# Half-swapped q and k by a partition shuffle out of PSUM, in place of two projections

## The chip, the cores and the metric

The kernel runs on one core of a Trainium2 chip. Its time is the device time of one execution in microseconds (us). A core has engines with instruction streams of their own: TensorE (PE, with PEld for its weight loads), VectorE (DVE), ScalarE (ACT), GpSimd (POOL) and SyncE (SP), which here only starts transfers. They meet by semaphores. Matmul results land in PSUM, which has eight banks of 128 partitions x 512 floats; GpSimd works on SBUF alone.

## The reference

An attention layer and a layer of experts, each behind a layer norm and with a residual, on x of 8 batches x 512 tokens x 128 channels, all float32. The attention has 16 heads of 8 channels, is causal, and turns q and k by rotary tables:

```python
def _rotate_half(x):
    x = x.reshape(x.shape[:-1] + (-1, 2))
    x1, x2 = (x[..., 0], x[..., 1])
    return jnp.stack((-x2, x1), axis=-1).reshape(x.shape[:-2] + (-1,))

def _apply_rope(x, cos, sin):
    return x * cos[None, None] + _rotate_half(x) * sin[None, None]
...
q, k, v = jnp.split(qkv, 3, axis=-1)
q = _apply_rope(q, cos, sin)
k = _apply_rope(k, cos, sin)
att = jnp.einsum('bhqd,bhkd->bhqk', q, k) * (1.0 / jnp.sqrt(...))
```

So each channel of q and k is needed once as it is, times a cosine, and once from its neighbour in the pair, times a signed sine. The expert layer (Sinkhorn gates over 8 experts, the top 64 tokens of each, one 128x128 matmul an expert) follows when all batches have been through the attention; the change doesn't touch it.

## The kernel before

**Layout.** q and k of a batch are projected transposed: 128 channels on the partitions, 512 tokens along them. The channels are ordered by (d, half, pair), d being the place within a head, so that the neighbour d ^ 1 of a channel lies 16 partitions away, within the same group of 32. `WQKV` holds the weights in that order, and `WSWAP` the same columns with d ^ 1 in place of d. `ROPE[:, 0..3]` holds cos and signed sin for q (scaled), then for k.

**A batch** is worked off in four groups of four heads, s = 0 to 3. For each group every engine goes through the list `STEP`, which is written out by hand and sets the order:

```python
STEP = [("w", 8), ("n", 0), ("n", 1), ("v", 0), ("u", 0), ("w", 9), ("x", 0), ("u", 1), ("u", 2),
        ("v", 3), ("u", 3), ("mx", 0), ("v", 1), ("v", 2), ("u", 4), ("c", 0), ("x", 1), ("u", 5),
        ("c", 1), ("u", 6), ("c", 2), ("x", 2), ("u", 7), ("c", 3), ("c", 4), ("c", 5), ("x", 3),
        ("ot", 0), ("c", 6), ("u", 8), ("c", 7), ("u", 9), ("x", 4)]
```

"u" is a unit of score rows for the next group (PE, L446), whose row maxima the vector engine takes (L895). A unit may start when an earlier unit's maxima are done (`BACK`); u3 waits for those of u0. "n" is minus_max on the vector engine (L906, L909), "mx" the transposes of the negated maxima (L494) and ACT's copy. "c" is a chunk of transposed scores (L459), which ACT exponentiates (L702); "w" are chunks 8 and 9 of the group before. GpSimd zeroes the acausal part of each diagonal chunk (`causal`, L812). "v" are the products with the values (L471); v0 needs two of a group's eight zeroed pieces, v1 and v3 six, and v2 all eight, the last two of which come from the chunks w8 and w9. "ot" transposes the outputs of the group before (L479). "x" are places for the extras.

**The extras** are the projections and the like, for the next batch (n) or for the one before (p). In group 0 stand at x1 the transposed input (xnT), at x2 q, at x3 qs, at x4 k; in group 1 at x0 ks. qs and ks are the projections with WSWAP. All of these and mx, ot and others share one PSUM bank, MB, in one order: each user on PE waits for `misc_free` to reach its number, which the reader of the one before raises.

**The rotation.** `turn` on the vector engine multiplies a projection out of MB by its table into TC (cos) or TS (sin) and frees the bank (L888). `rotate` on GpSimd adds TC and TS into RES[w], w = 0 for q, 1 for k (L796); in its order it stands behind c4 of group 0 for q and behind u2 of group 1 for k. RES is then cut into three bf16 parts (ACT L696 and DVE L876, with subtractions on GpSimd, L800), which SP stores to memory and loads back as the operands of the score matmuls of the next batch.

**The loop.** Batch 0 and batch 7 are written out, batches 1 to 6 are three turns of a loop of two. Batch 7 prepares no next one. The first q and k, for batch 0, are made before this by code of their own (`first_turn`, `first_sum`), which uses both weight arrays.

Of the kernel before, what the change touches and what calls it, by code (L numbers as in the profile page):

```python
# [10 lines left out]
ALU = mybir.AluOpType  # L11
AX = mybir.AxisListType

B, T, C = 8, 512, 128
H, HD = 16, 8
E = 8
P = 128
# [31 lines left out]
LAST_V = [i for kind, i in STEP if kind == "v"][-1]  # L49

EXTRAS = {(0, 1): "xnT n", (0, 2): "q n", (0, 3): "qs n", (0, 4): "k n", (1, 0): "ks n",
          (1, 1): "yT p", (1, 2): "proj p", (1, 3): "v n", (2, 4): "xn2T p", (3, 2): "logits p"}

ROTATE = {(0, "c", 4): 0, (1, "u", 2): 1}
CUT = {(1, "x", 0): (0, 0), (1, "v", 1): (1, 0), (1, "c", 1): (1, 1), (1, "u", 6): (0, 1),
       (1, "x", 3): (1, 2)}
CUT_V = {(1, "c", 4): (0, 2)}
# [88 lines left out]
def build(nc, x_in, w_qkv, w_swap, w_proj, gate_w, experts, rope, tri, ident, small, out):  # L148
    ctx = ExitStack()
    with ctx:  # L150
        def sb(name, shape, dt=F32):
            return ctx.enter_context(nc.sbuf_tensor(name, shape, dt))
# [25 lines left out]
        WSWAP = sb("WSWAP", [P, 2 * C])  # L178
# [3 lines left out]
        ROPE = sb("ROPE", [P, 4, T])  # L182
# [17 lines left out]
        MV = sb("MV", [P, B * TB, 2])  # L200
        RSTD = sb("RSTD", [P, B * TB])
        SHIFT = sb("SHIFT", [P, B * TB])
        TC = sb("TC", [P, T])
        TS = sb("TS", [P, T])
        RES = [sb(f"RES{w}", [P, T]) for w in range(2)]
        PARTS = [sb(f"PARTS{w}", [P, 3, T], BF16) for w in range(2)]

# [49 lines left out]
        MB = ctx.enter_context(nc.psum_tensor("MB", [P, T], F32))  # L257
# [3 lines left out]
        FIRSTB = ROWP + CH[0:2]  # L261
# [27 lines left out]
        misc_free = sem("misc_free")  # L289
# [6 lines left out]
        resid = [sem("q_residual"), sem("k_residual")]  # L296
# [132 lines left out]
        def _(pe):  # L429
# [73 lines left out]
            def project(bt, name, weight):  # L503
                misc(bt, name)
                pe.matmul(MB[:, :], weight, XNT[:, :], start=True, stop=True).then_inc(misc_full, 1)  # L505

            def q(bt): project(bt, "q", WQKV[:, 0:C])
            def qs(bt): project(bt, "qs", WSWAP[:, 0:C])
            def k(bt): project(bt, "k", WQKV[:, C:2 * C])
            def ks(bt): project(bt, "ks", WSWAP[:, C:2 * C])  # L510

            def by_tiles(bt, name, src, weight, n):
                misc(bt, name)
# [13 lines left out]
                transposes(lambda t: XN2[:, t, :]).then_inc(misc_full, 1)  # L527
            def logits(bt): by_tiles(bt, "logits", XN2S, WGATE[:, :], E)

            extras = {"xnT": xn_transposed, "q": q, "qs": qs, "k": k, "ks": ks, "v": v,  # L530
                      "yT": y_transposed, "proj": proj, "xn2T": xn2_transposed, "logits": logits}

            pe.wait_ge(ident_loaded, 16)
# [6 lines left out]
            for t in range(TB):  # L540
                last = pe.matmul(FIRSTB[4][:, C * t:C * t + C], XNT[:, P * t:P * t + P], WQKV[:, 2 * C:3 * C],
                                 start=True, stop=True)
# [232 lines left out]
        @block.gpsimd  # L775
        def _(pool):
            pool.memset(NHALF[:, :], -0.5)
            pool.memset(ONES[:, :], 1.0).then_inc(built, 1)

            def rstd(n, stats, mv, dst, shift, done):  # L780

                pool.wait_ge(stats, n)
                pool.nop(nofuse=True)
                pool.tensor_scalar(dst, mv[:, :, 1], LN_EPS, None, ALU.add)
                pool.tensor_scalar(shift, mv[:, :, 0], -1.0, None, ALU.mult)
                pool.drain()
                pool.tensor_tensor(dst, dst, NHALF[:, 0:dst.shape[1]], ALU.pow)
                pool.drain()
                pool.tensor_tensor(shift, shift, dst, ALU.mult).then_inc(done, 1)  # L789

            def rotate(bt, w):
                b = bt.b + 1
                pool.wait_ge(misc_free, bt.misc(("qs", "ks")[w]) + 1)
                if not (isinstance(b, int) and b == 0):
                    pool.wait_ge(part[w], 3 * b)
                pool.tensor_tensor(RES[w][:, :], TC[:, :], TS[:, :], ALU.add).then_inc(resid[w], 1)  # L796

            def subtract(b, w, i):
                pool.wait_ge(part[w], 3 * b + i + 1)
                pool.tensor_tensor(RES[w][:, :], RES[w][:, :], PARTS[w][:, i, :], ALU.subtract).then_inc(resid[w], 1)  # L800

            def causal(b, s, z):

                c = z + 2 if z >= 2 else 2 * z + 1
                pool.wait_ge(exp_done, 4 * NC * b + NC * s + c + 1)
                pool.nop(nofuse=True)
                if z < 2:
                    v = PT[s % 2][:, c - 1:c + 1, 0:P]
                else:
                    cols = [col // P for _, _, col in CHUNKS[c]]  # L810
                    v = PT[s % 2][:, c, :].rearrange("p (a t) -> p a t", a=TB)[:, 0:TB:cols[1] - cols[0], :]
                pool.affine_select(out=v, in_=v, pattern=[[0, 2], [1, P]], compare_op=ALU.is_ge, fill=0.0,  # L812
                                   base=0, channel_multiplier=-1).then_inc(causal_done, 1)

            rstd(1, ln_stats, MV[:, 0:TB], RSTD[:, 0:TB], SHIFT[:, 0:TB], ln_rstd)
            pool.memset(ONER[:, :], 1.0).then_inc(built, 1)
            for i in range(2):
                pool.memset(KZ[i][1][:, :, :].rearrange("p a t -> p (a t)").bitcast(U32), 0).then_inc(built, 1)
            rstd(2, ln_stats, MV[:, TB:], RSTD[:, TB:], SHIFT[:, TB:], ln_rstd)

            def one(bt):
                for s in range(4):
                    for kind, i in STEP:
                        vb, vs = (bt.b, s - 1) if s > 0 else (bt.b - 1, 3)
                        if kind == "c" and (i >= 4 or i % 2 == 1):
                            causal(bt.b, s, i - 2 if i >= 4 else i // 2)
                        if kind == "w" and (s > 0 or bt.prev):
                            causal(vb, vs, i - 2)
                        if bt.nxt and (s, kind, i) in ROTATE:
                            rotate(bt, ROTATE[s, kind, i])  # L830
                        if bt.nxt and (s, kind, i) in SUBTRACT:
                            subtract(bt.b + 1, *SUBTRACT[s, kind, i])
                        if bt.prev and (s, kind, i) == RSTD2_AT:
                            rstd(bt.b, ln2_stats, MV2, RSTD2[:, :], SHIFT2[:, :], ln2_rstd)

            batches(pool, one)
            causal(B - 1, 3, 6)
            causal(B - 1, 3, 7)
            rstd(B, ln2_stats, MV2, RSTD2[:, :], SHIFT2[:, :], ln2_rstd)


            order = [(b, t) for b in range(DIRECT) for t in OTHERS[b]]
            for j, (b, t) in enumerate(order):
                x = X[:, TB * b + t, :]
                pool.wait_ge(weighted, j + 1)
                pool.tensor_tensor(SUM4[:, :, :], WY[j % 2][:, 0:4, :], WY[j % 2][:, 4:8, :], ALU.add).then_inc(folded, 1)  # L846
                pool.wait_ge(folded, 4 * j + 1)
                pool.tensor_tensor(SUM2[:, :, :], SUM4[:, 0:2, :], SUM4[:, 2:4, :], ALU.add).then_inc(folded, 1)  # L848
                pool.wait_ge(folded, 4 * j + 2)
                pool.tensor_tensor(SUM1[:, :], SUM2[:, 0, :], SUM2[:, 1, :], ALU.add).then_inc(folded, 1)  # L850
                pool.wait_ge(folded, 4 * j + 3)
                pool.tensor_tensor(x, SUM1[:, :], x, ALU.add).then_inc(folded, 1)
# [3 lines left out]
        def _(dve):  # L856
# [18 lines left out]
                    dve.wait_ge(stored[w], 48 * b)  # L875
                dve.tensor_copy(PARTS[w][:, i, :], RES[w][:, :]).then_inc(part[w], 1)  # L876

            def turn(bt, name, i, w, dst):

                b = bt.b + 1  # L880
                if i % 2 == 0:

                    if w == 1:
                        dve.wait_ge(resid[0], 3 * b + 1)
                    elif not (isinstance(b, int) and b == 0):
                        dve.wait_ge(resid[1], 3 * b - 2)
                dve.wait_ge(misc_full, bt.misc(name) + 1)
                dve.tensor_tensor(dst[:, :], MB[:, :], ROPE[:, i, :], ALU.mult).then_inc(misc_free, 1)  # L888

            def row_maxima(b, s, u):  # L890
                dve.wait_ge(rows_ready, 4 * NU * b + NU * s + u + 1)
# [41 lines left out]
            def clip_logits(bt):  # L933
# [1 line left out]
                dve.tensor_scalar(LG[:, bass.ds(4 * (bt.b - 1), TB), :].rearrange("p t e -> p (t e)"),  # L935
                                  MB[:, 0:TB * E], CLIP_EPS, None, ALU.max).then_inc(misc_free, 1)

            extras = {"q": lambda bt: turn(bt, "q", 0, 0, TC), "qs": lambda bt: turn(bt, "qs", 1, 0, TS),
                      "k": lambda bt: turn(bt, "k", 2, 1, TC), "ks": lambda bt: turn(bt, "ks", 3, 1, TS),
                      "proj": add_attention, "logits": clip_logits}  # L940

            dve.wait_ge(x_first, 16)
# [12 lines left out]
            def first_turn(i):  # L955
                dve.wait_ge(first_full, i + 1)
                if i == 2:
                    dve.wait_ge(resid[0], 1)
                last = dve.tensor_tensor((TC, TS)[i % 2][:, :], FIRSTB[i], ROPE[:, i, :], ALU.mult)
                if i % 2 == 1:  # L960
                    last.then_inc(first_turned, 1)

            def first_sum(w):
                dve.wait_ge(first_turned, w + 1)
                dve.tensor_tensor(RES[w][:, :], TC[:, :], TS[:, :], ALU.add).then_inc(resid[w], 1)

            def first_cut(w, i):
                dve.wait_ge(resid[w], i + 1)
# [260 lines left out]
```

## Time and profile before

| | |
|---|---|
| median of 3 runs | 553.68 us (552.65 to 554.0) |
| the profiled execution | 556.51 us |
| its span in the trace | 554.8 us |
| busy: PE / DVE / ACT / POOL | 432.3 / 419.3 / 331.3 / 232.2 us |
| attention loop, one batch | 45.96 us, 49.30 us with the loop's branch in it |

The rows come from one profiled execution. A span is the time from the first to the last record of the core; an execution takes a little longer than that. Busy time of an engine is that of its instructions and can overlap a little where one begins as another drains. In the timeline a bracket behind a row says how long the engine had stood idle before it, and which instruction it then waited for.

### The profile page before, as it was taken

How to read it: one execution, taken by the hardware profiler on the slowest of the kernel's cores; microseconds unless marked ns; L12 is line 12 of the kernel's file. 1: busy time of each engine (PE TensorE's matmuls, PEld its weight loads, DVE VectorE, ACT ScalarE, POOL GpSimd, SP SyncE). 2: the span in 40 equal slices, each digit the busy share in tenths (PEclk: the TensorE clock that was granted, in tenths of full speed). 3: DMA queues.
4: the chain of work that ended last, by engine and by line, in shares of the span. 5: the costliest groups of instructions: out<-in, count | busy, mean ns of one | idle time of the engine just before them, and what ended most of it. 6: DMA issues, size and time to landing. Idle time of an engine off the chain costs nothing.

```text
span 554.8 us, 11459 instructions
## 1 busy us (share of the span) xinstructions
PE 432.3 (78%) x2985; PEld 219.7 (40%) x2985; DVE 419.3 (76%) x1693; ACT 331.3 (60%) x660; POOL 232.2 (42%) x399
## 2 busy tenths in 40 slices
PE   0507989989998898998989899899987778898200
PEld 0202445454554445445444554545543333343100
DVE  7777668778878768877867887778951699889980
ACT  0002568677868657877775887768693324328613
POOL 5121453363365236336424633633342000009997
PEclk9955879999999989999999999989999799899755
DMA  8570052035026004402600520360010100101111
GB/s 255 138 180 0 30 158 44 1 115 135 2 94 136 22 0 141 105 1 95 151 2 28 152 66 0 114 132 2 2 58 0 40 19 19 39 0 38 39 45 48
DMA packets 28108, 36.72 MB, mean 66 GB/s; under 512 B 2072, under 2 KB 24088, under 8 KB 26392
## 3 DMA queue, kind: packets, MB, share of 16 engines
q1 hardware_dynamic: 27120, 34.68, 22.7%
q10 hardware_dynamic: 944, 1.57, 1.1%
q8 instruction: 13, 0.21, 0.2%
q14 instruction: 31, 0.25, 0.2%
HBM read 19.41 MB, written 16.78 MB: 65 GB/s over the span
## 4 chain that ended last, share of the span: by engine, by line
PE 54%; DVE 13%; ACT 10%; POOL 10%; issue 9%; DMA 2%; DVEq 1%; POOLq 1%; ACTq 1%
PE ROWB L446 12%; PE PVB L471 12%; PE CHB L459 11%; PE MB L505 5%; PE MB L479 5%; ACT YS L702 4%; POOL SUM L848 4%; POOL SUM L846 3%; PE MB L515 3%; PE MB L494 3%; PE ROWB L643 2%; ACT XN L681 1%; DVE XN L946 1%; DMA parts_scratch<-PARTS 1%; POOL SUM L850 1%
## 5 line engine op out<-in xcount | busy, mean ns | idle before, releaser
L895 DVE CUSTOM_DVE_ANT_0 JUNK<-ROWB,TRI 128x384 bf16<-128x384 f32 (+3 forms) x512 | 221.2, 487 | 41.0 <-PE ROWB L446 39.6
L702 ACT ACTIVATE YS<-CHB 128x512 f32<-128x512 f32 x320 | 171.9, 607 | 56.9 <-PE CHB L459 56.8
L812 POOL TENSOR_SCALAR_AFFINE_SELECT YS<-YS 128x256 f32<-128x256 f32 x256 | 104.6, 413 | 178.7 <-ACT YS L702 170.1
L446 PE MATMUL ROWB<-YS 96*128 96x384 bf16 (+3 forms) x512 | 123.4, 314 | 24.0 <-DMA YS<-parts_scratch 17.7
L459 PE MATMUL CHB<-YS 100*128 100x384 bf16 (+3 forms) x512 | 118.3, 308 | 12.9 <-ACT YS L702 11.0
L471 PE MATMUL PVB<-YS,VP 128*32 128x512 f32 (+3 forms) x1024 | 97.0, 452 | 0.2 <-POOL YS L812 0.2
L446 PEld LDWEIGHTS ROWB<-YS 96*128 96x128 bf16 x512 | 43.3, 100 | 101.6 <-DVE MX L895 57.2
L459 PEld LDWEIGHTS CHB<-YS 100*128 100x128 bf16 x512 | 46.3, 100 | 48.0 <-ACT YS L702 19.4
L656 ACT ACTIVATE YS<-MB 4x1024 bf16<-4x1024 bf16 x32 | 32.5, 1017 | 38.6 <-PE MB L494 38.5
L771 ACT ACTIVATE YS<-YS,W 128x128 f32<-128x128 f32 x104 | 31.5, 388 | 35.6 <-POOL SUM L846 18.9
L846 POOL TENSOR_TENSOR SUM<-YS 128x512 f32<-128x512 f32 x13 | 16.9, 1298 | 70.1 <-ACT YS L771 70.1
L471 PEld LDWEIGHTS PVB<-YS,VP 128*32 128x32 f32 x1024 | 35.1, 110 | 27.5 <-POOL YS L812 13.0
L895 DVE DVE_READ_ACCUMULATOR2_ANT MX<- 128x1 f32 x512 | 42.5, 83 | 0.0
L800 POOL TENSOR_TENSOR RES<-RES,PARTS 128x512 f32<-128x512 f32 x28 | 31.8, 1157 | 12.7 <-ACT PARTS L696 12.7
L593 PE MATMUL CHB<-WEXP,XS 128*128 128x512 f32 x58 | 28.8, 601 | 2.1 <-DVE X L1171 2.1
L593 PE MATMUL ROWB<-WEXP,XS 128*128 128x512 f32 x58 | 30.0, 625 | 0.0
L479 PE MATMUL MB<-IDF,OT 128*128 128x128 f32 x128 | 20.9, 287 | 11.1 <-ACT VP L666 6.1
L479 PE MATMUL MB<-IDF,XN 128*128 128x128 f32 x64 | 11.9, 316 | 18.7 <-DVE XN L946 16.0
L917 DVE RECIPROCAL RSUM<-MB 128x16 f32<-128x16 f32 x32 | 8.2, 257 | 24.0 <-PE MB L479 24.0
L848 POOL TENSOR_TENSOR SUM<-SUM 128x256 f32<-128x256 f32 x13 | 22.2, 1704 | 1.0
L673 ACT ACTIVATE XN<-X,SHIFT,RSTD 128x128 f32 (+1 forms) x28 | 11.5, 482 | 18.6 <-POOL SHIFT L789 18.6
L696 ACT ACTIVATE PARTS<-RES 128x512 bf16<-128x512 f32 x35 | 21.6, 640 | 0.4 <-POOL RES L800 0.3
(124 smaller groups left out, 568.7 us busy)
## 6 DMA issues: line engine op xcount, KB each, us to landing
YS<-parts_scratch SPq DMA_DIRECT2D x30, 384.0 KB, 6.4
parts_scratch<-PARTS SPq DMA_DIRECT2D x15, 384.0 KB, 2.5
parts_scratch<-PARTS SPq DMA_DIRECT2D x15, 256.0 KB, 2.2
X<-in_x SPq DMA_DIRECT2D x8, 256.0 KB, 5.7
xn_scratch<-XN2S SPq DMA_DIRECT2D x8, 256.0 KB, 2.0
XS<-xn_scratch SPq DMA_DIRECT2D x8, 256.0 KB, 2.6
out<-X SPq DMA_DIRECT2D x8, 256.0 KB, 2.3
parts_scratch<-PARTS SPq DMA_DIRECT2D x15, 128.0 KB, 1.7
```

The costliest lines, as they stand in the source:

```text
L446: last = pe.matmul(ROWP[BANK[u]][:, col:col + keys], QP[par][0:ROWS_K, pair, P * qb:keys], KZ[par][i % 2][0:ROWS_K, pair, 0:keys], start=T ...
L459: last = pe.matmul(CH[BANK[c]][:, col:col + n], KZ[par][i % 2][0:ALL_K, pair, P * kb:P * kb + P], QP[par][0:ALL_K, pair, P * kb:T], start= ...
L471: last = pe.matmul(PVB[32 * i:32 * i + 32, P * kb:T], VP[par][:, v:v + 32], PT[s % 2][:, c, col:col + T - P * kb], start=(kb == 0), stop=( ...
L479: last = pe.transpose(MB[:, P * t:P * t + P], src(t), IDF[:, :])
L593: last = pe.matmul(buffer(n, half), XS[b % 2][:, P * t:P * t + P], WEXP[:, 4 * half:4 * half + 4, :].rearrange("p e o -> p (e o)"), start= ...
L656: act.activation(dst, src, ACT.Copy).then_inc(misc_free, 1)
L702: act.activation(PT[s % 2][:, c, :], CH[BANK[c]], ACT.Exp).then_inc(exp_done, 1)
L800: pool.tensor_tensor(RES[w][:, :], RES[w][:, :], PARTS[w][:, i, :], ALU.subtract).then_inc(resid[w], 1)
L812: pool.affine_select(out=v, in_=v, pattern=[[0, 2], [1, P]], compare_op=ALU.is_ge, fill=0.0, base=0, channel_multiplier=-1).then_inc(causa ...
L846: pool.tensor_tensor(SUM4[:, :, :], WY[j % 2][:, 0:4, :], WY[j % 2][:, 4:8, :], ALU.add).then_inc(folded, 1)
L848: pool.tensor_tensor(SUM2[:, :, :], SUM4[:, 0:2, :], SUM4[:, 2:4, :], ALU.add).then_inc(folded, 1)
L895: last = dve.tensor_tensor_reduce(out=JUNK[BANK[u]][:, col:col + n], in0=ROWP[BANK[u]][:, col:col + n], in1=TRI[:, T - n:T], scale=1.0, sc ...
```

## The change

q and k are each projected once. The vector engine reads the bank twice: it multiplies by the cosine table into TC[w], and then a stream shuffle with the permutation `TURN` (i to i ^ 16 within each group of 32 partitions) copies the half-swapped projection into TS[w] and frees the bank. GpSimd multiplies TS[w] by the sine table in place and, after a drain, adds TC[w] and TS[w]. TC and TS become two buffers each. k takes the place x3 of qs; x4 of group 0 and x0 of group 1 are empty. The second rotation stands behind x4 of group 0, and not behind u2 of group 1. The code ahead of batch 0 keeps its four projections.

```diff
-EXTRAS = {(0, 1): "xnT n", (0, 2): "q n", (0, 3): "qs n", (0, 4): "k n", (1, 0): "ks n",
-          (1, 1): "yT p", (1, 2): "proj p", (1, 3): "v n", (2, 4): "xn2T p", (3, 2): "logits p"}
-ROTATE = {(0, "c", 4): 0, (1, "u", 2): 1}
+EXTRAS = {(0, 1): "xnT n", (0, 2): "q n", (0, 3): "k n", (1, 1): "yT p", (1, 2): "proj p", (1, 3): "v n", (2, 4): "xn2T p",
+          (3, 2): "logits p"}
+ROTATE = {(0, "c", 4): 0, (0, "x", 4): 1}
+TURN = [i ^ 16 for i in range(32)]
...
-        TC = sb("TC", [P, T])
-        TS = sb("TS", [P, T])
+        TC = [sb(f"TC{w}", [P, T]) for w in range(2)]
+        TS = [sb(f"TS{w}", [P, T]) for w in range(2)]
...
             def rotate(bt, w):
                 b = bt.b + 1
-                pool.wait_ge(misc_free, bt.misc(("qs", "ks")[w]) + 1)
+                pool.wait_ge(misc_free, bt.misc("qk"[w]) + 1)
+                pool.nop(nofuse=True)
+                pool.tensor_tensor(TS[w][:, :], TS[w][:, :], ROPE[:, 2 * w + 1, :], ALU.mult)
+                pool.drain()
                 if not (isinstance(b, int) and b == 0):
                     pool.wait_ge(part[w], 3 * b)
-                pool.tensor_tensor(RES[w][:, :], TC[:, :], TS[:, :], ALU.add).then_inc(resid[w], 1)
+                pool.tensor_tensor(RES[w][:, :], TC[w][:, :], TS[w][:, :], ALU.add).then_inc(resid[w], 1)
...
-            def turn(bt, name, i, w, dst):
+            def turn(bt, name, w):
                 b = bt.b + 1
-                if i % 2 == 0:
-                    if w == 1:
-                        dve.wait_ge(resid[0], 3 * b + 1)
-                    elif not (isinstance(b, int) and b == 0):
-                        dve.wait_ge(resid[1], 3 * b - 2)
+                if not (isinstance(b, int) and b == 0):
+                    dve.wait_ge(resid[w], 3 * b - 2)
                 dve.wait_ge(misc_full, bt.misc(name) + 1)
-                dve.tensor_tensor(dst[:, :], MB[:, :], ROPE[:, i, :], ALU.mult).then_inc(misc_free, 1)
+                dve.tensor_tensor(TC[w][:, :], MB[:, :], ROPE[:, 2 * w, :], ALU.mult)
+                dve.stream_shuffle(TS[w][:, :], MB[:, :], TURN).then_inc(misc_free, 1)
```

## Rows read from the trace of the kernel before

**Rows 1.** The page: the span, and the chain that ended last by engine and line.
```profile
span 554.8 us, 11459 instructions
...
PE 54%; DVE 13%; ACT 10%; POOL 10%; issue 9%; DMA 2%; DVEq 1%; POOLq 1%; ACTq 1%
PE ROWB L446 12%; PE PVB L471 12%; PE CHB L459 11%; PE MB L505 5%; PE MB L479 5%; ACT YS L702 4%; POOL SUM L848 4%; POOL SUM L846 3%; PE MB L515 3%; PE MB L494 3%; PE ROWB L643 2%; ACT XN L681 1%; DVE XN L946 1%; DMA parts_scratch<-PARTS 1%; POOL SUM L850 1%
```

**Rows 2.** Windows of one batch: length, engines' busy time, clock, DMA share, GB/s.
```profile
149.22:198.52 49.30, 43.75 (x350) 23.21 (x349) 36.82 (x162) 35.20 (x69) 21.74 (x42) 0.97 0.26 71
198.52:244.48 45.96, 42.13 (x350) 22.68 (x349) 37.04 (x162) 35.15 (x69) 21.76 (x42) 1.00 0.28 75
```

**Rows 3.** Groups by line: projections and rotation; busy us, mean ns, idle before.
```profile
L796 POOL TENSOR_TENSOR RES<-TC,TS 128x512 f32<-128x512 f32 x14 | 17.8, 1273 | 8.8 <-DVE TS L888 8.8
...
L505 PE MATMUL MB<-XNT,WQKV 128*128 128x512 f32 x28 | 16.4, 670 | 0.0
L505 PE MATMUL MB<-XNT,WSWAP 128*128 128x512 f32 x28 | 15.1, 619 | 0.0
```

**Rows 4.** Timeline, batch from 198.5, around q, qs, ot: start us, us, what.
```profile
199.63 0.69 DVE L888 TENSOR_TENSOR TC<-MB,ROPE 128x512 f32<-128x512 f32 x1
...
200.37 1.12 PE L505 MATMUL MB<-XNT,WSWAP 128*128 128x512 f32 x2
...
200.79 0.90 POOL L812 TENSOR_SCALAR_AFFINE_SELECT YS<-YS 128x256 f32<-128x256 f32 x2 [1.35 <-ACT YS L702]
...
201.54 0.69 DVE L888 TENSOR_TENSOR TS<-MB,ROPE 128x512 f32<-128x512 f32 x1 [0.53 <-PE MB L505]
...
202.36 0.65 PE L479 MATMUL MB<-IDF,OT 128*128 128x128 f32 x4 [0.86 <-DVE TS L888]
...
203.27 1.09 ACT L702 ACTIVATE YS<-CHB 128x512 f32<-128x512 f32 x2 [1.63 <-PE CHB L459]
...
203.51 0.38 PE L446 MATMUL ROWB<-YS 96*128 96x256 bf16 x2
...
210.13 0.39 PE L446 MATMUL ROWB<-YS 96*128 96x384 bf16 x2
```

**Rows 5.** Timeline, the stretch from u9 to u4 one group later.
```profile
217.86 0.38 PE L446 MATMUL ROWB<-YS 96*128 96x256 bf16 x2
...
219.46 0.30 DVE L906 TENSOR_SCALAR NMX<-MX 128x16 bf16<-128x16 f32 x1
...
220.00 0.69 DVE L895 CUSTOM_DVE_ANT_0 JUNK<-ROWB,TRI 128x512 bf16<-128x512 f32 x1
...
220.76 0.39 PE L446 MATMUL ROWB<-YS 96*128 96x512 bf16 x1
...
221.52 1.24 PE L471 MATMUL PVB<-YS,VP 128*32 128x384 f32 x13
...
222.70 0.39 PE L446 MATMUL ROWB<-YS 96*128 96x384 bf16 x2
```

**Rows 6.** Casts to bf16: beside POOL's subtractions (timeline), and alone (ns min/median/max).
```profile
214.03 2.27 POOL L800 TENSOR_TENSOR RES<-RES,PARTS 128x512 f32<-128x512 f32 x2 [0.49 <-ACT PARTS L696]
...
215.22 1.36 DVE L876 CAST PARTS<-RES 128x512 bf16<-128x512 f32 x1
...
L969 DVE CAST PARTS<-RES x6: 415/426/427, 23.1 to 29.8; 128x512 bf16<-128x512 f32 x6
```

**Rows 7.** Timeline, POOL: an instruction behind a drain.
```profile
222.78 1.05 POOL L787 TENSOR_TENSOR RSTD<-RSTD,NHALF 128x4 f32<-128x4 f32 x1 [0.15 <-issue]
```

**Rows 8.** Windows of slow clock (columns as in rows 2), and PE's idle times.
```profile
193.66:197.07 3.41, 3.41 (x26) 1.72 (x23) 1.28 (x5) 1.61 (x2) 0.00 (x0) 0.50 0.00 0
74.20:81.02 6.82, 5.95 (x27) 2.70 (x26) 3.36 (x13) 3.29 (x9) 3.13 (x7) 0.50 0.47 110
...
193.03 0.39 PE L446 MATMUL ROWB<-YS 96*128 96x512 bf16 x1 [2.00 <-DVE MX L895]
...
73.00 0.34 PE L459 MATMUL CHB<-YS 100*128 100x384 bf16 x1 [1.51 <-ACT YS L702]
...
226.54 0.34 PE L459 MATMUL CHB<-YS 100*128 100x384 bf16 x1 [1.18 <-ACT YS L702]
```

More of the change, by code:

```diff
@@ L507, in q @@
             def q(bt): project(bt, "q", WQKV[:, 0:C])
-            def qs(bt): project(bt, "qs", WSWAP[:, 0:C])
             def k(bt): project(bt, "k", WQKV[:, C:2 * C])
-            def ks(bt): project(bt, "ks", WSWAP[:, C:2 * C])
             def by_tiles(bt, name, src, weight, n):
@@ L528, in logits @@
             def logits(bt): by_tiles(bt, "logits", XN2S, WGATE[:, :], E)
-            extras = {"xnT": xn_transposed, "q": q, "qs": qs, "k": k, "ks": ks, "v": v,
+            extras = {"xnT": xn_transposed, "q": q, "k": k, "v": v,
                       "yT": y_transposed, "proj": proj, "xn2T": xn2_transposed, "logits": logits}
@@ L936, in clip_logits @@
                                   MB[:, 0:TB * E], CLIP_EPS, None, ALU.max).then_inc(misc_free, 1)
-            extras = {"q": lambda bt: turn(bt, "q", 0, 0, TC), "qs": lambda bt: turn(bt, "qs", 1, 0, TS),
-                      "k": lambda bt: turn(bt, "k", 2, 1, TC), "ks": lambda bt: turn(bt, "ks", 3, 1, TS),
+            extras = {"q": lambda bt: turn(bt, "q", 0), "k": lambda bt: turn(bt, "k", 1),
                       "proj": add_attention, "logits": clip_logits}
@@ L958, in first_turn @@
                     dve.wait_ge(resid[0], 1)
-                last = dve.tensor_tensor((TC, TS)[i % 2][:, :], FIRSTB[i], ROPE[:, i, :], ALU.mult)
+                last = dve.tensor_tensor((TC, TS)[i % 2][0][:, :], FIRSTB[i], ROPE[:, i, :], ALU.mult)
                 if i % 2 == 1:
@@ L964, in first_sum @@
                 dve.wait_ge(first_turned, w + 1)
-                dve.tensor_tensor(RES[w][:, :], TC[:, :], TS[:, :], ALU.add).then_inc(resid[w], 1)
+                dve.tensor_tensor(RES[w][:, :], TC[0][:, :], TS[0][:, :], ALU.add).then_inc(resid[w], 1)
             def first_cut(w, i):
```

## The prediction

> **What bounds the kernel now.** I read the page first, its span and the chain of work that ended last [rows 1]. TensorE (PE) carries 54% of that chain, VectorE (DVE) 13%, ScalarE (ACT) 10% and GpSimd (POOL) 10%. The line of the projections, L505, is 5.0% of it: 27.7 us of the 31.5 us that those matmuls are busy. So the removed work lies nearly all on the path. Then I cut the attention loop into batches [rows 2]: a batch takes 45.96 us, or 49.30 us where it holds the loop's branch, and PE is busy for about 92% of the first kind. PE sets the pace, in an order written out by hand, and DVE, ACT and POOL follow closely. What a removed matmul is worth depends on who is next behind PE at that place, so I read the timeline of one batch around the changed lines [rows 4] and the same stretch one group of heads later, which has no projection there [rows 5].
>
> **What is removed.** Of the four projections of a batch, the two with WSWAP. L505 shows 28 rows for 14 such projections, two passes each, 15.1 us in all [rows 3]. What they cost where they stand is read by comparison. From the score rows u9 to the score rows u4 PE takes 210.13 - 203.51 = 6.62 us in the stretch that holds two projections [rows 4], and 222.70 - 217.86 = 4.84 us in the stretch that holds none [rows 5]. So 1.78 us a batch of PE time goes there. (q stays at x2; k moves from x4 to x3, the old place of qs.)
>
> **What is added on the shared PSUM bank.** All these results pass through the one bank MB, and the bank is freed by the vector engine's last read. Before, that was one multiply after each projection: the multiply of q started at 199.63 and PE's next projection at 200.37; the multiply of qs started at 201.54 and the transposes of "ot" at 202.36, PE idle for 0.86 us [rows 4]. Now q and k each are read twice, multiply and shuffle, before the bank is free. No row of before shows a shuffle. Its nearest row is the multiply of the same 128x512 from PSUM, 0.69 us [rows 4]; two such instructions one after the other follow at 0.60 to 0.69 us. I take 0.65; the bounds are 0.42 (the fastest 128x512 pass of this engine in the trace, a cast inside SBUF [rows 6]) and 1.36 (the slowest, the same cast beside POOL [rows 6]). PE waits at both places already, so both additions are on its path: k starts at 201.02, ot at 202.36 + 1.30 = 203.66. PE then stands idle from 202.14 to 203.66, 1.52 us. Net so far: 1.30 - 1.78 = -0.48 us a batch. DVE's own load does not change: two multiplies out, two shuffles in.
>
> The Trainium skill (VectorE: DVE Perf Modes, the perf-mode tier table) gives a stream shuffle of 2048 columns about 2400 ns and knows no faster mode for it. Scaled to 512 columns that is an estimate of 0.60 us, and with it the net would be -0.58 instead of -0.48.
>
> **What is added on POOL.** Each of the two rotations was one addition of 1.27 us [rows 3]. Now there is a multiply of the same shape before it, and a drain between; a drained successor follows 0.15 us later [rows 7]. A rotation is then 1.27 + 0.15 + 1.27 = 2.69 us. Behind it in POOL's queue stand the causal selects, and PE's value products wait for these. I walk POOL with PE's new times. The selects of c3 and c4 end at 201.69 [rows 4], and q's bank is free by then, so rotation 0 runs 201.7 to 204.4. The exponentials of c6 and c7, before at 203.27 for 1.09 us [rows 4], move by 1.30 and end at 205.66, so the last select ahead of x4 ends at about 206.19 (I allow 0.12 for its start, and it is 0.41 long). Rotation 1, now at (0,"x",4), runs 206.2 to 208.9. The selects of w8 and w9, which v2 needs, are queued behind it and end at 209.7. Would PE be there earlier? By the stretch without projections it reaches u4 4.84 us after u9, that is at 204.81 + 4.84 = 209.65, and v2 is the last eight of the 13 instructions in front of it [rows 5], 0.7 us: v2 would start at 208.95. It waits 0.8 us, and u4 comes at about 210.5, where before it came at 210.13: +0.37 us a batch. A multiply on POOL as fast as its quickest such row would win back at most a few tenths; at nothing for it, the -0.48 stands.
>
> **What the longer rotation blocks on DVE.** The first step of minus_max, L906, comes 1.60 us after u9 [rows 5], at 206.41, just after the new multiply has begun on POOL. What happens then is in the rows: the same cast takes 0.426 us alone [rows 6] and 1.36 us beside POOL's subtractions, and L906 beside a select took 0.30 us [rows 5]. So it is held to the end of POOL's instruction, 207.46, and u0's maxima start at 207.75 where 206.95 was possible. Unit u3 needs them: u0's maxima at 220.00, u3 at 220.76 [rows 5], with PE already waiting for DVE. So u3 comes at 208.5 in place of 207.7 and v2 again at 209.75. The two delays fall on the same gap and aren't added. This rests on rows of before alone.
>
> The Trainium skill (SBUF: State Buffer, "SBUF: two separate sides") says the same as a rule that speaks against this change: the pair of ports that the vector engine and GpSimd share is an exclusive lock, held for a whole instruction, and the loser blocks fully. The trace agrees: 1.36 against 0.426 us. By that rule each multiply moved to GpSimd costs the vector engine up to 1.27 us wherever it wants the pair; it is rival 3 below.
>
> Other edits. Taking ks and the k turn from their old places frees DVE there, which has slack already. RES[1] is ready some tenths of a microsecond earlier, but the cut into parts waits for its place in ACT's order, so nothing is gained. The second pair TC/TS removes two waits that found their semaphore already set. SP's and the DMA queues get no new instruction, and the part stores move with PE.
>
> **The clock.** PE's granted clock fell to 0.50 (1.2 GHz) at 193.66, after an idle time of 2.00 us that ended at 193.03, and at 74.20 after one of 1.51 us that ended at 73.00; after one of 1.18 us it stayed at 2.4 GHz [rows 8]. The new wait before ot is 1.52 us, with 0.5 us of idle before k and 0.8 us before u3 or v2. The price comes from the batches: 49.30 - 45.96 = 3.34 us for one with the branch [rows 2], less the 2.00 us of idle, leaves 1.3 us for the slow clock. I take three falls in the seven batches, 3.9 us.
>
> **The sum.** Seven of eight batches prepare a next one. 7 x 0.37 = 2.6 us and 3 x 1.3 = 3.9 us: +6.5 us on the span of 554.8 us. The profiled execution took 556.51 us, 1.7 us around its span, and that part does not change; the median of the runs is 553.68 us, 2.8 us under it, and I put the difference on the median: 560.2 us.
>
> **Rivals.**
> 1. The same waits, but the clock holds: +2.6 us, 556.3 us. For it: 1.18 us of idle left the clock alone. Against: 1.51 us did not. Chance 0.22; my forecast with falling clock in two batches or more has 0.33.
> 2. It ends faster: PE's saving stays and POOL is hidden. This decides where the rotation takes POOL under about 1.9 us or the selects of w8 and w9 otherwise come before v2: -0.48 x 7 = -3.4 us, 550.3 us; with a shuffle that overlaps the multiply by half, -1.1 x 7, 546 us. For it: POOL is busy for only 21.8 of 45.96 us [rows 2]. Against: the idle time lies elsewhere in the batch. Chance 0.18.
> 3. The port lock catches both steps of minus_max, the second behind POOL's addition: u0's maxima start at 209.0 or later, u3 at 209.8, u4 1.6 us later than before, 7 x 1.6 = 11.2 us and falls of the clock with it, 4 x 1.3: 570 us. In my walk the second step wins by under 0.1 us. Chance 0.10.
> 4. Nothing measurable: the waits just equal the saving, 553.7 us. Chance 0.17.
>
> **The numbers.** From no change, 0.3% (1.7 us) can be told on this kernel. Faster by more is rival 2, 0.18; within it rival 4, 0.17; slower by more the rest, 0.65. The range reaches from 549.0 us, a little under rival 2's first case, to 568 us, short of rival 3 whole. The range of the slower cases alone is 555.5 to 565.
>
> **What the profile after would show.** A shuffle near 0.69 us after each multiply from MB; PE idle before ot of 1.4 to 1.6 us in place of 0.86; POOL rows of 1.27 us in pairs, a select of w8 directly behind the second; v2 or u3 waiting for POOL or DVE by some 0.8 us; L906 at s = 1 at over 1 us; more falls of PEclk between 104 and 350 us. It would be wrong if the shuffle runs beside the multiply, if v2 never waits for POOL, or if the clock stays up.

## The result and the profile after

The changed kernel takes 561.5 us (median of 4 runs, 558.95 to 564.92), the kernel before 553.84 us on the same chip; the ratio is 1.0121 with a 95% interval of 1.0077 to 1.0166. It is slower by 1.2%, though TensorE does 28 passes less. The profiled execution took 560.62 us. Some executions of a kernel run in a slower state, at a lower granted clock and over 1.5% above the fastest; the ratios leave those out.

The page after: span, busy times, the chain that ended last by engine and line.
```profile
span 558.9 us, 11421 instructions
...
PE 422.2 (76%) x2957; PEld 215.5 (39%) x2957; DVE 424.7 (76%) x1707; ACT 331.0 (59%) x660; POOL 249.1 (45%) x413
...
PE 48%; DVE 16%; issue 11%; ACT 10%; POOL 10%; DMA 2%; DVEq 1%; POOLq 1%; ACTq 1%
```
TensorE's share of the chain fell from 54% to 48% and the vector engine's rose from 13% to 16% [rows 1]. The removed work was on the path, and waits took its place.

Windows of two batches after, the first with the loop's branch, the second without it and without a clock fall.
```profile
249.99:299.31 49.32, 41.98 (x345) 22.64 (x345) 37.78 (x162) 35.32 (x69) 24.13 (x44) 0.97 0.26 70
299.31:345.50 46.19, 40.35 (x346) 21.70 (x345) 37.84 (x162) 34.96 (x69) 24.15 (x44) 1.00 0.28 74
```
The window of the same batch before, from its q projection to the next:
```profile
293.39:339.24 45.85, 42.02 (x349) 22.57 (x348) 37.09 (x160) 35.06 (x69) 21.77 (x42) 1.00 0.27 75
```
So PE is busy for 1.67 us less and the batch is 0.34 us longer. The last q projection stands at 345.50, 6.3 us later than before. The span is only 4.1 us longer: some 2 us come back after that projection, 1.6 us of them because the profile before has a fall of the clock at 367.7 us and the profile after has none there.

The groups of the projection, of the shuffle and of the rotation after (busy us, mean ns | idle before).
```profile
L798 POOL TENSOR_TENSOR RES<-TC,TS 128x512 f32<-128x512 f32 x14 | 17.8, 1270 | 2.4 <-issue 1.3
L794 POOL TENSOR_TENSOR TS<-TS,ROPE 128x512 f32<-128x512 f32 x14 | 17.8, 1269 | 0.0
L506 PE MATMUL MB<-XNT,WQKV 128*128 128x512 f32 x28 | 16.4, 670 | 3.7 <-DVE TS L887 3.7
...
L887 DVE STREAM_SHUFFLE TS<-MB 128x512 f32<-128x512 f32 x14 | 10.2, 730 | 0.0
...
L887 DVE LOAD_MASK_SELECT TS<-MB x14 | 0.2, 14 | 0.0
```
The 15.1 us of the WSWAP projections are gone. The shuffle takes 0.73 us, the loading of its mask 14 ns, and POOL's multiply 1.27 us, as the addition does.

The timeline after, batch from 250.0, from the multiply of q to u4.
```profile
251.15 0.69 DVE L886 TENSOR_TENSOR TC<-MB,ROPE 128x512 f32<-128x512 f32 x1
...
251.77 0.73 DVE L887 STREAM_SHUFFLE TS<-MB 128x512 f32<-128x512 f32 x1
...
252.55 1.13 PE L506 MATMUL MB<-XNT,WQKV 128*128 128x512 f32 x2 [0.56 <-DVE TS L887]
...
253.18 1.27 POOL L794 TENSOR_TENSOR TS<-TS,ROPE 128x512 f32<-128x512 f32 x1
...
254.65 1.27 POOL L798 TENSOR_TENSOR RES<-TC,TS 128x512 f32<-128x512 f32 x1 [0.21 <-issue]
...
255.19 0.66 PE L480 MATMUL MB<-IDF,OT 128*128 128x128 f32 x4 [1.51 <-DVE TS L887]
...
256.34 0.38 PE L447 MATMUL ROWB<-YS 96*128 96x256 bf16 x2
...
257.69 1.27 POOL L794 TENSOR_TENSOR TS<-TS,ROPE 128x512 f32<-128x512 f32 x1
...
257.94 1.06 DVE L905 TENSOR_SCALAR NMX<-MX 128x16 bf16<-128x16 f32 x1
...
259.03 0.18 DVE L908 SCALAR_TENSOR_TENSOR NMX<-MX,NMX 128x16 bf16<-128x16 f32 x1
...
259.11 1.26 POOL L798 TENSOR_TENSOR RES<-TC,TS 128x512 f32<-128x512 f32 x1
...
259.24 0.69 DVE L894 CUSTOM_DVE_ANT_0 JUNK<-ROWB,TRI 128x512 bf16<-128x512 f32 x1
...
259.99 0.39 PE L447 MATMUL ROWB<-YS 96*128 96x512 bf16 x1 [0.72 <-DVE MX L894]
...
260.33 0.76 POOL L814 TENSOR_SCALAR_AFFINE_SELECT YS<-YS 128x256 f32<-128x256 f32 x2
...
260.96 1.02 ACT L655 ACTIVATE YS<-MB 4x1024 bf16<-4x1024 bf16 x1 [1.32 <-PE MB L495]
...
261.14 0.38 PEld L472 LDWEIGHTS PVB<-YS,VP 128*32 128x32 f32 x8 [0.27 <-POOL YS L814]
...
261.93 0.39 PE L447 MATMUL ROWB<-YS 96*128 96x384 bf16 x2
```
These answer to [rows 4] and [rows 5]. The bank is freed by the shuffle, so PE stands 0.56 us before k and 1.51 us before ot (0.86 before the change). The multiply of rotation 1 starts at 257.69, minus_max 0.25 us later, and its first step, 128x16 elements, takes 1.06 us: it ends when the multiply does. PE waits 0.72 us before u3 for what follows it. GpSimd's queue is hardly earlier: its selects of w8 and w9 end at 261.09, and the weights of v2 load at 261.14, after 0.27 us of waiting for them. From u9 to u4 it is 5.59 us in place of 6.62.

Windows of slow clock after.
```profile
107.41:110.83 3.42, 3.35 (x18) 2.30 (x22) 1.71 (x9) 1.27 (x3) 1.70 (x4) 0.50 0.00 0
206.40:213.23 6.83, 6.55 (x27) 2.91 (x27) 4.19 (x15) 2.23 (x4) 4.96 (x7) 0.50 0.00 0
```
Of the stretches that began between 80 and 400 us, six had the clock at 0.50 (1.2 GHz) after the change, 23.9 us together, against three and 10.2 us before. The two shown began at 107.4 and 206.4 us, just before ot's transposes (107.48 and 206.68), at the end of PE's wait; a third of this kind began at 155.2 us, 0.5 us after that wait. The other three have counterparts before: two at the loop's branch, and one in group 2 (at 179.1 us, before at 367.7 us).

### The profile page after: what moved, and what is told of

The parts are those of the page before. It is cut to its first block, busy times and chain, and to the rows that moved or that the text cites. A ratio compares the mean times of both kernels' runs of the same rounds, so it can differ in the third digit from the quotient of the medians.

```text
span 558.9 us, 11421 instructions
## 1 busy us (share of the span) xinstructions
PE 422.2 (76%) x2957; PEld 215.5 (39%) x2957; DVE 424.7 (76%) x1707; ACT 331.0 (59%) x660; POOL 249.1 (45%) x413
## 4 chain that ended last, share of the span: by engine, by line
PE 48%; DVE 16%; issue 11%; ACT 10%; POOL 10%; DMA 2%; DVEq 1%; POOLq 1%; ACTq 1%
PE ROWB L447 11%; PE PVB L472 11%; PE CHB L460 9%; PE MB L480 5%; ACT YS L701 5%; POOL SUM L850 4%; POOL SUM L848 3%; PE MB L506 3%; PE MB L514 3%; PE MB L495 3%; DVE TS L887 2%; DVE JUNK L894 2%; PE ROWB L642 2%; ACT XN L680 1%; DVE XN L944 1%
## 5 line engine op out<-in xcount | busy, mean ns | idle before, releaser
L460 PEld LDWEIGHTS CHB<-YS 100*128 100x128 bf16 x512 | 46.2, 100 | 43.9 <-ACT YS L701 18.7
L480 PEld LDWEIGHTS MB<-IDF,OT 128*128 128x128 f32 x128 | 14.2, 146 | 23.5 <-issue 7.8
```

What stands on the lines that cost most here:

```text
L460: last = pe.matmul(CH[BANK[c]][:, col:col + n], KZ[par][i % 2][0:ALL_K, pair, P * kb:P * kb + P], QP[par][0:ALL_K, pair, P * kb:T], start= ...
L480: last = pe.transpose(MB[:, P * t:P * t + P], src(t), IDF[:, :])
```

## The experiments

A useful measure is the step from one group to the next, between two of ScalarE's copies of the negated maxima (rows `4x1024`, one a group). In batches 2, 4 and 6 of the loop a step repeats to 0.02 us where the clock does not fall; in 1, 3 and 5, which follow the loop's start or its branch, it is up to 0.15 us longer. This table has the value of batches 2, 4 and 6 without a fall of the clock, from the profile of each kernel, with the times of the runs. Each ratio is to the kernel before on the same chip, whose medians there were 553.6 to 555.0 us:

| kernel | group 0 to 1 | 1 to 2 | both | median us | ratio to before (95%) |
|---|---|---|---|---|---|
| before | 13.33 | 12.56 | 25.9 | 553.84 | |
| changed | 13.68 | 12.57 | 26.25 | 561.5 | 1.0121 (1.0077 to 1.0166) |
| e1 | 12.93 | 13.66 | 26.6 | 565.52 | 1.0199 (1.0156 to 1.0242) |
| e2 | 11.40 | 13.52 | 24.9 | 544.57 | 0.9815 (0.9771 to 0.9860) |
| e3 | 12.64 | 12.57 | 25.2 | 549.66 | 0.9888 (0.9819 to 0.9957) |
| e4 | 13.67 | 12.56 | 26.2 | 554.91 | 1.0001 (0.9974 to 1.0027) |
| e5 | 11.40 | 12.44 | 23.85 | 539.4 | 0.9723 (0.9669 to 0.9777) |
| e6 | 11.75 | 12.43 | 24.2 | 541.01 | 0.9752 (0.9699 to 0.9805) |
| e7 | 12.88 | 13.38 | 26.26 | 564.86, one run | |
| e8 | 13.69 | 12.57 | 26.26 | 559.14, one run | |
| e9 | 13.34 | 12.56 | 25.9 | 555.41 | 1.0019 (0.9987 to 1.0051) |
| e10 | 11.40 | 12.44 | 23.85 | 541.12 | 0.9776 (0.9740 to 0.9811) |

(In e1 and e7 the step 1 to 2 also has shorter values, 13.43 to 13.50 in e1 and 12.57 in e7. These follow a step with a slow clock; it ends later, and with it the wait that comes after is shorter or gone.)

**e1, the second rotation back at its old place.**
```diff
-ROTATE = {(0, "c", 4): 0, (0, "x", 4): 1}
+ROTATE = {(0, "c", 4): 0, (1, "u", 2): 1}
```


> The changed kernel with the second rotation back behind u2 of group 1, where it stood before the change; nothing else differs. Theory A (port lock): the 0.72 us that TensorE waits before u3 is gone, because minus_max no longer meets the new multiply on GpSimd (its first step takes under 0.3 us again, where it took 1.06), and a batch without a clock fall goes from 46.2 to 45.5 us; ScalarE's cut of RES[1] may now wait for the later rotation, up to 0.5 us. About 557 us, against 561.5. Rival B (GpSimd's length alone matters, wherever the rotation stands): no gain, 561 us. Rival C (only the clock matters): the falls stay as many and the time stays within 1 us.

The timeline of e1, same stretch: minus_max, u3, the late rotation, and what waits for it.
```profile
257.98 0.31 DVE L905 TENSOR_SCALAR NMX<-MX 128x16 bf16<-128x16 f32 x1
...
259.29 0.39 PE L447 MATMUL ROWB<-YS 96*128 96x512 bf16 x1
...
261.09 1.27 POOL L798 TENSOR_TENSOR RES<-TC,TS 128x512 f32<-128x512 f32 x1
...
262.39 0.63 ACT L695 ACTIVATE PARTS<-RES 128x512 bf16<-128x512 f32 x1 [1.12 <-POOL RES L798]
...
264.67 1.16 PE L514 MATMUL MB<-WPROJ,YT 128*128 128x128 f32 x8 [1.52 <-ACT YT L655]
```
The lock part came as expected: minus_max 0.31 us, no wait before u3, step 0 to 1 shorter by 0.75 us. The time went the other way, a miss: RES[1] is now ready at 262.36, ScalarE stands 1.12 us before its cut, its copy of yT is late, and proj waits 1.52 us where it waited 0.43. Step 1 to 2 grows by 1.09 us. I had put this at 0.5 us, and as a wait of ScalarE that costs PE less. So the earlier place of the rotation, which meets minus_max, was also what kept the longer rotation out of the cuts' way. The expected 557 us was missed by 8 us, and neither rival had this cause.

**e2, k at x4 as well.**
```diff
-EXTRAS = {(0, 1): "xnT n", (0, 2): "q n", (0, 3): "k n", (1, 1): "yT p", ...
-ROTATE = {(0, "c", 4): 0, (0, "x", 4): 1}
+EXTRAS = {(0, 1): "xnT n", (0, 2): "q n", (0, 4): "k n", (1, 1): "yT p", ...
+ROTATE = {(0, "c", 4): 0, (1, "u", 2): 1}
```


> As e1, and k projected at x4 as before the change, so that no user of the shared PSUM bank stands right behind it. Theory A (the second read of the bank is on TensorE's path): the wait of 1.5 us before ot shrinks to about 0.5 us (ot now follows q's shuffle, after three chunks), the wait of 0.56 us before k is gone, and the clock has no reason to fall there: a batch of about 44.5 us, 7 x 1.7 = 12 us under the changed kernel's clean batches, 543 to 547 us in all, faster than the kernel before. Rival (the vector engine is the limit after all): minus_max, now behind multiply and shuffle of k, comes 0.7 us later and TensorE waits before u3 and mx for it; 551 to 555 us.

544.57 us, 1.85% faster than before and within the 543 to 547 us expected. Nothing but the place of k and of its rotation differs from the changed kernel, and 17 us lie between them. The clean batch is shorter by 1.3 us, which is 9 us in seven batches. The rest fits the clock: the profile of e2 has no slow stretch that began between 80 and 400 us, the changed kernel's has six. Step 0 to 1 is 11.40 us: 1.93 us under before. The matmuls of u9 to u4 had been priced at 1.78 us a batch; with the wait before ot cut from 0.86 to 0.56 us the rest is explained within 0.2 us.

**e3, the bank freed by the multiply.** cos is the same for the two channels of a pair, so the shuffle can read TC, and the tangent takes the place of the sine.
```diff
-                dve.tensor_tensor(TC[w][:, :], MB[:, :], ROPE[:, 2 * w, :], ALU.mult)
-                dve.stream_shuffle(TS[w][:, :], MB[:, :], TURN).then_inc(misc_free, 1)
+                dve.tensor_tensor(TC[w][:, :], MB[:, :], ROPE[:, 2 * w, :], ALU.mult).then_inc(misc_free, 1)
+                dve.drain()
+                dve.stream_shuffle(TS[w][:, :], TC[w][:, :], TURN).then_inc(turned[w], 1)
...
-                pool.tensor_tensor(TS[w][:, :], TS[w][:, :], ROPE[:, 2 * w + 1, :], ALU.mult)
+                pool.tensor_tensor(TS[w][:, :], TS[w][:, :], TAN[:, :], ALU.mult)
```


> The changed kernel with the bank freed by the multiply: the shuffle reads TC (q times cosine) in SBUF, and GpSimd multiplies by the tangent in place of the sine. Orders and places are those of the changed kernel. Theory A: TensorE's waits before k and ot fall back from 0.56 and 1.5 us to under 0.2 and about 0.86 us, 1.2 us a batch, with fewer falls of the clock; the port lock stays. About 561.5 - 7 x 1.2 - 2 = 551 us. Rival (the waits only move): TensorE comes earlier and waits before v2 or u3 for GpSimd and the vector engine instead; 558 to 561 us.

549.66 us, as expected (551): 11.8 us under the changed kernel. Step 0 to 1 is 1.04 us shorter, with ot's wait at 0.99 us and no wait before k. The lock has moved to minus_max's second step.

The timeline of e3: both steps of minus_max, the multiply that holds the second, and u3.
```profile
247.08 0.28 DVE L909 TENSOR_SCALAR NMX<-MX 128x16 bf16<-128x16 f32 x1
...
247.30 1.27 POOL L797 TENSOR_TENSOR TS<-TS,TAN 128x512 f32<-128x512 f32 x1
...
247.39 1.21 DVE L912 SCALAR_TENSOR_TENSOR NMX<-MX,NMX 128x16 bf16<-128x16 f32 x1
...
249.26 0.39 PE L450 MATMUL ROWB<-YS 96*128 96x512 bf16 x1 [0.85 <-DVE MX L898]
```
Seven times 1.04 is 7.3 us. The remaining 4.5 us are in no clean step; the clock is what is left, and the profile has three slow stretches that began between 80 and 400 us, 10.2 us together, in place of six and 23.9 us.

**e4, the wait before ot filled with matmuls.**
```diff
             def out_transposed(bt, b, s, name):
+                pe.wait_ge(pv_copied, 4 * b + s + 1)
+                if s == 3 and bt.nxt and bt.prev and name == "ot3":
+                    for _ in range(5):
+                        pe.matmul(PVB[:, :], KZ[bt.par][0][0:ROWS_K, 0, 0:P], QP[bt.par][0:ROWS_K, 0, :],
+                                  start=True, stop=True)
                 misc(bt, name)
-                pe.wait_ge(pv_copied, 4 * b + s + 1)
```


> The changed kernel with five bf16 matmuls of 512 columns into the idle values bank, in batches 1 to 6, put where TensorE waits 1.5 us before ot; their results are not used. Theory A (clock): they fit into the wait (about 1.1 us), ot starts when it did or up to 0.1 us later, the clock no longer falls between q and v2 of a batch, and the time is 3 to 4 us less, 558 us. Rival (the clock falls have another cause, or cost nothing): 561 to 563 us with as many falls.

The timeline of e4: the projection of k, the filling, ot.
```profile
244.24 1.13 PE L510 MATMUL MB<-XNT,WQKV 128*128 128x512 f32 x2 [0.56 <-DVE TS L891]
...
245.20 1.24 PE L487 MATMUL PVB<-YS 96*128 96x512 bf16 x5
...
246.87 0.66 PE L480 MATMUL MB<-IDF,OT 128*128 128x128 f32 x4 [0.43 <-DVE TS L891]
```
Work that nobody uses makes the kernel 1.2% faster: 554.91 us. The clean step is the same to 0.01 us, so the 6.6 us are the clock's. Its profile has a single slow stretch that began between 80 and 400 us, where the changed kernel has six. Expected were 3 to 4 us. The gain is not the same in every run: two of the ten, 561.05 and 564.87 us at mean granted clocks of 0.914 and 0.908, are not in the ratio. With them the mean of all ten is 556.1 us, 5.6 us under the changed kernel's mean of 561.7.

**e9, the control**, the kernel before with three filling matmuls in its own wait of 0.86 us (the same edit with three in place of five).

> A control for e4: the kernel before with three such filling matmuls, about 0.65 us, in its own wait of 0.86 us before ot, batches 1 to 6. Theory A (the filling works through the clock alone): the kernel before has no falls between q and ot to lose, its falls come at the loop's branch and after the waits of 1.2 us, so the time stays within 1 us of 554. Rival (the filling helps or harms in some way of its own, whatever the clock): the time moves by several us, as it did between the changed kernel and e4.

Ratio 1.0019 (0.9987 to 1.0051): the filling gives the kernel before nothing that can be measured. What it gave the changed kernel belongs to the wait that the change made longer. (One of the twelve runs, 559.68 us, is not in the ratio.)

**e7 and e8, two sides of the port.** e7 adds `pool.wait_ge(nmax_ready, 4 * bt.b + 2)` ahead of the second rotation; e8 leaves out the multiply and its drain, so its q and k are not those of the reference, and only its times are read. Each was run once; what is read are the clean steps of its profile.

> The changed kernel with one wait more: the second rotation on GpSimd starts only when minus_max of group 1 is done. The port lock is gone (minus_max's first step under 0.45 us), and the selects of w8 and w9 end later, by about 0.6 us. If GpSimd's queue was a limit of its own as the prediction had it, TensorE now waits before v2 in place of u3, by about 1.0 us, and the step from group 0 to 1, 13.68 us without a clock fall in the changed kernel, becomes 13.9 to 14.1 us. If only the lock counted, it falls to 12.95 us as in e1.

> The changed kernel without GpSimd's multiply by the sine (the addition takes the unmultiplied TS, so q and k are not those of the reference). Theory A (the lock by whatever instruction GpSimd runs when minus_max comes): the second addition now stands where the multiply stood and holds minus_max just as long, u3 waits 0.7 us as before, and the clean step from group 0 to 1 stays 13.68 us. Rival (the doubled work on GpSimd is what costs): it falls by 0.5 us or more, to 13.2 us or less.

The timeline of e7: minus_max free, the rotation behind it, and v2.
```profile
258.04 0.18 DVE L907 TENSOR_SCALAR NMX<-MX 128x16 bf16<-128x16 f32 x1
...
260.00 1.28 POOL L800 TENSOR_TENSOR RES<-TC,TS 128x512 f32<-128x512 f32 x1
...
261.23 0.78 POOL L816 TENSOR_SCALAR_AFFINE_SELECT YS<-YS 128x256 f32<-128x256 f32 x2
...
262.05 0.64 PE L472 MATMUL PVB<-YS,VP 128*32 128x256 f32 x8 [1.17 <-POOL YS L816]
```
The timeline of e8: one addition, and minus_max beside it.
```profile
256.23 1.26 POOL L796 TENSOR_TENSOR RES<-TC,TS 128x512 f32<-128x512 f32 x1
...
256.47 1.06 DVE L903 TENSOR_SCALAR NMX<-MX 128x16 bf16<-128x16 f32 x1
...
258.55 0.39 PE L447 MATMUL ROWB<-YS 96*128 96x512 bf16 x1 [0.73 <-DVE MX L892]
```
In e7 the wait before u3 is gone and a wait of 1.17 us before v2 has come, as expected. I had looked for it in the wrong step: the copy that marks the step comes ahead of v2, so it shows in 1 to 2. The two steps together are 26.26 us, as in the changed kernel. So a wait for GpSimd's queue has taken the place of the lock, with the same sum. Part of it is the edit's own: the rotation starts 0.8 us later here. But in the changed kernel too, v2's weights load only when GpSimd's selects end (0.05 us after, above), so by these rows the queue would hold v2 there if the lock were gone. e8 says the same from the other side. Without the multiply, the clean steps are 13.69 and 12.57 us, unchanged; the addition moved forward into minus_max's way and holds it for the same 1.06 us. With the lock there, the doubled work on GpSimd adds nothing to the step; what costs is that one of its instructions begins just ahead of minus_max.

**e5, e6, e10, after a faster kernel.** e5 is e2 with the cuts of group 1 put later:
```diff
-CUT = {(1, "x", 0): (0, 0), (1, "v", 1): (1, 0), (1, "c", 1): (1, 1), (1, "u", 6): (0, 1), (1, "x", 3): (1, 2)}
+CUT = {(1, "x", 0): (0, 0), (1, "x", 1): (1, 0), (1, "c", 2): (0, 1), (1, "x", 2): (1, 1), (1, "x", 3): (1, 2)}
-SUBTRACT = {(1, "u", 2): (1, 0), (1, "u", 3): (0, 0), (1, "c", 1): (0, 1), (1, "u", 6): (1, 1)}
+SUBTRACT = {(1, "u", 3): (0, 0), (1, "c", 0): (1, 0), (1, "x", 2): (0, 1), (1, "u", 7): (1, 1)}
```
(`PART_ORDER` follows the same order.) e6 adds the edit of e3, e10 the filling of e4: two matmuls before ot of group 0, five before ot of group 1.

> As e2 (k at x4, its rotation behind u2), and ScalarE's cuts and GpSimd's subtractions of group 1 put later: the first cut of k behind the copy of yT at x1, no longer at v1. Theory A: in e1 and e2 ScalarE stood 1.0 us before the first cut of k, since RES[1] comes later than before, and its copy of yT and TensorE's proj waited for that (1.4 us of idle in place of 0.43). Then the group 1 to group 2 step of 13.53 us falls back to 12.57 us, 7 x 0.96 = 6.7 us: 538 us, against 544.6 for e2. Rival (the lengthening comes from elsewhere, or a later cut makes a wait of its own): 543 to 546 us.

> As e5, with the bank freed by the multiply as in e3 (shuffle out of TC, tangent on GpSimd). Theory A: TensorE's wait before ot, 0.56 to 0.64 us in e2, nearly vanishes: 7 x 0.5 = 3.5 us under e5, 535 us. Rival: TensorE then waits for something else in the same stretch, the exponentials or unit u3, and the time stays that of e5 within 1 us.

> e5, the fastest so far, with filling matmuls in its two longest regular waits outside the loop's branch: two before ot of group 0 (wait 0.6 us), five before ot of group 1 (wait 1.4 us), batches 1 to 6. Theory A: the clock falls near 170 and 262 us go, each worth 1.2 to 1.6 us: 1.5 to 3 us less than e5, 537 us. Rival: those falls come from the 1.18 us wait in group 2, which is not filled, and the time stays at 539 to 540 us.

e5: 539.4 us (538 expected), 2.8% faster than before, and step 1 to 2 is back at 12.44 us; that settles where e1 and e2 lost their microsecond. Two misses follow. In e6 the wait before ot is gone, but step 0 to 1 is 0.35 us longer and PE waits 0.44 us before u3: multiply, drain and shuffle of k end later now and stand right in front of minus_max. e10 gains nothing over e5 (541.12 against 539.4 us, intervals overlap): its profile has falls of the clock at 128 and 264 us, at the end of PE's wait of 1.2 us in group 2, which was not filled, so the rival of that run has the cause right (its 539 to 540 us were 1 us too low). In e5 too the two falls outside the branch, at 170.7 and 262.8 us, began within 0.3 us of the start of PE's work after that wait, and none began at the longer waits of 1.41 to 1.45 us before ot of group 1. So the filled waits had no falls to lose there.

## Why the prediction was right

560.2 us was predicted and 561.5 measured. The waits were right one by one. In the two profiles the falls of the clock came out as summed, too. How the 7.7 us between the medians divide is known only in part, and some luck is in how close 560.2 came.

**What is removed** was on the path. e2 gives back 1.93 us in the step that had held both projections, against 1.78 us priced.

**The bank.** The projection at x3 (k, before it was qs) comes 1.40 us after the start of q's multiply, against 0.74 before: +0.66, predicted +0.65. ot comes 4.04 us after it, against 2.73 before: +1.31, predicted +1.30. Idle before ot: 1.51, predicted 1.52. The shuffle is 0.73 us and starts 0.62 us after the multiply's start, near the rows that I had taken for it. e3 supports the price: with the bank free early 1.04 us of the 1.30 a batch come back, while u3's wait grows from 0.72 to 0.85 us.

**GpSimd and the lock.** A rotation takes 2.74 us (253.18 to 255.92), predicted 2.69. minus_max's first step 1.06 us, as walked, and u3's wait 0.72 us, predicted 0.8. That the queue's wait and the lock's fall on one gap is borne out by e7 (26.26 us, against 26.25 with the lock). From q's multiply to u4 it is 10.78 us, against 10.50 before: +0.28, predicted +0.37. The clean batch grew by 0.34 us. The second step of minus_max was not caught (rival 3): L908 starts 0.08 us ahead of POOL's addition, the margin of the walk. How thin that margin is shows in e3, where the second step is held for 1.21 us.

By the Trainium skill (SBUF: State Buffer, "SBUF: two separate sides") one instruction holds the shared port pair for its whole length, and the loser fully blocks until then; the trace agrees, with 1.06 us for an operation that takes 0.18 us alone, ending 0.04 us after the multiply. e8 adds that the length of GpSimd's queue does not matter for this, only which instruction holds the pair at that moment.

**The clock.** "Three falls in the seven batches, 3.9 us" is what the profiles show: six slow stretches in place of three, at the price put on them. The three that began at the new waits lie in step 0 to 1 of batches 1, 2 and 3. These steps take 14.86, 14.50 and 17.24 us, against 13.48, 13.33 and 15.02 before (the last with the fall at the loop's branch in both); less the clean growth of 0.35 us each, that is 3.7 us. A fall in step 2 to 3 costs 1.6 us (12.07 against 10.47) in both kernels. The reason given for the falls was too simple, though: only three of the six waits of 1.5 to 1.6 us before ot in batches 1 to 6 have one. And the profile before, from which one wait of 1.18 us with the clock up was quoted, also has a fall after one of 1.19 us, at 367.7 us, which I overlooked.

**The sum.** Step by step, batches 1 to 6 together grew by 6.0 us in the profiles: 6 x 0.35 = 2.1 us clean, nearly all the rest clock; the prediction's terms give 6 x 0.37 + 3.9 = 6.1 us. Batch 0, which I charged like the others, took 45.0 us in place of 46.2, without the fall at 74 us of the profile before, and what comes after the loop is 0.9 us shorter (0.2 us more lie ahead of batch 0). So the span grew by 4.1 us, where 6.5 us was predicted.

The medians differ by 7.7 us, 3.6 us more than the spans. The profiled execution of the kernel before was 2.7 us over its median, that of the changed kernel 0.9 us under its own. The extra microseconds are thus in runs without a profile, of which only the mean granted clock is on record: 0.911, 0.905, 0.914 and 0.920 for 560.62, 564.92, 562.39 and 558.95 us. The longest run has the lowest clock and the shortest the highest, so the spread goes with the clock. The kernel before had a mean of 0.919 in 37 recorded runs, in which the time rose by about 3.2 us where the clock was 0.01 lower. By that, an estimate, the changed kernel's mean of 0.9125 is worth 2 us. e4 gives more: 5.6 to 6.6 us for what the wait before ot does to the clock, with the control e9 at no change. Between these two figures the clock's share of the 7.7 us stays open, beside 2.4 us (7 x 0.34) for the clean batches. Also open is why the clock falls after one wait and not after another of the same length; the traces only show that it does.

## What to carry to other kernels

When work is taken off the engine that sets the pace, look at who frees the buffer behind it: here a second reader of one PSUM bank put 1.3 us back where 1.8 us were removed, and moving one projection by six entries of a list, with its rotation put back to its old place, turned a loss of 1.2% into a gain of 1.9%. Before an operation is moved to GpSimd, look at what small operation the vector engine will want through the shared port at that moment, rather than at how busy GpSimd is. And look at what the granted clock does behind a wait on TensorE that a change makes longer: here filling the wait with unused matmuls, which shortened no clean step, gave back 5.6 to 6.6 us, where the clean batches had lost 2.4 us in all.

## What the runs showed of the hardware

A stream shuffle of 128x512 floats out of PSUM takes 0.73 us, and out of SBUF 0.73 to 0.74 us (e3); its mask load takes 14 ns. Five matmuls whose result nobody reads, in a wait of 1.5 us, made the kernel faster by 6.6 us (medians) through the clock alone. An operation of the vector engine on 128x16 elements, 0.18 us alone, takes 1.06 us beside a GpSimd addition or multiply of 1.27 us that began just before it. Waits of one length did not always do the same to the clock: in the kernel before it fell at 367.7 us after one of 1.19 us and stayed up after five others of 1.18 us. In e2 it stayed up after all six waits of 1.39 to 1.46 us before proj.
